# A DLRM tower with a two-layer interaction network: a top layer in two banks, a masked product, loads on two queues and a ninth pair of table products

## The chip, the cores and the metric

The kernel runs on one core of one Trainium2 chip. The metric is the device time of one execution in microseconds (us). Before the change the median of three runs is 152.55 us (152.45 to 153.67).

## The reference

For each of 512 samples, 26 embedding rows of 32 numbers are looked up. Two interaction layers follow, each a sum over pairs of fields, then three dense layers:

```
e  = stack(tbl_f[ids[:, f]] for f in 0..25)                  # 512 x 26 x 32
x1 = einsum('bik,bjk,hij->bhk', e,  e, W1) + b1              # W1: 128 x 26 x 26
x2 = einsum('bik,bjk,hij->bhk', x1, e, W2) + b2              # W2: 128 x 128 x 26
z  = concat(sum_k x1, sum_k x2)                              # 512 x 256
h  = relu(concat(z, dense_ctx) @ W_top1 + b_top1)            # 272 -> 512
h  = relu(h @ W_top2 + b_top2)                               # 512 -> 256
y  = h @ W_top3                                              # 256 -> 1
```

## The kernel before

The batch is cut into four groups (g = 0 to 3) of 128 samples. The network is linear in its weights, so both layers are folded: once, at the start, weight tables are mixed into `v_in`, `v_ac` (for x2) and `wg` (for x1), and then each group only needs products of field pairs and triples, contracted with these tables.

**At the start.** SyncE's queue loads the indices, W2 and W1, index copies for a one-hot form (`octet`, 125 partitions), eight small embedding tables (`small_tbl`, 125 partitions each, four for fields of the second half, four for the first half), the context rows of the top layer eight times (`wt1c_in`, line 314) and the dense weights, in the order in which `sync` writes them (lines 302 to 318). VectorE clears buffers, splits the context (lines 366 to 378) and the context weights (`split_wt1c`, line 599) into three bf16 parts, prepares W1's tables (lines 383 to 409), and turns the index copies into one-hot matrices (`one_hot`, `one_hot_rest`). TensorE computes 26 products W2 x W1 (`mix`, line 667), ScalarE copies each out of PSUM.

**Embeddings.** GpSimd gathers one field of one group per indirect DMA (line 350), 88 in all, in the order of groups and fields. Fields in `OH_PAIRS` are not gathered: a pair of fields of a small table is looked up by TensorE as one-hot x table (`look_up`, line 714), then VectorE masks and sums the result (`pick`, line 519), two instructions a pair. `OH_AT` puts the look-ups of group g+1 behind two places of group g's transposed products; pairs beyond two come after the last of them.

**A group.** VectorE's `build_a` and `build_b` transpose the embeddings (`take_part`), copy them to `l`, multiply pairs, and fill `R` (`fill_r`, line 550), a block-diagonal form of the same numbers: each of four quarters of 32 partitions has its own slot. For groups 0 and 1 ScalarE fills `R` instead. `l` and `R` have one buffer, so `build_a` of a group waits for the products of the group before. TensorE's `t_block` (lines 684 to 712) contracts `l` with `R`, eight matmul blocks and then four more, into a ring of four PSUM banks; ScalarE copies each to `t_in` or `t_ac`. Then `z_group`: 26 products `inner` (line 746) on `t_in`, 13 products `across` (line 751) on `t_ac`, and `gram_part` (line 734), four products for x1. The operand of `gram_part` makes a detour: SyncE's queue writes rows of `t_in` to DRAM and reads them back as `gram` (lines 320 to 331) after the first eight blocks are copied out.

**The top.** ScalarE copies the two halves of z out of PSUM (`z_copy`), TensorE runs `layer1` (lines 786 to 794: four blocks m of 128 outputs, three matmuls each, all in bank `h1p`), ScalarE applies ReLU per block (`relu1`), TensorE runs `layer2` and, one block of the next group later, `layer3`. On TensorE `layer1` and `layer2` of group g stand between `z_group` of g and the first `t_block` of g+1. ScalarE's order in between is `z_copy(0)`, `fill_r(1, 1)`, `relu1(0)`, `fill_r(1, 2)` for group 0, and without the fills later.

Of the kernel before, what the change touches and what calls it, by code (L numbers as in the profile page):

```python
# [16 lines left out]
BF16 = mybir.dt.bfloat16  # L17
# [4 lines left out]
P = 128  # L22
NF = 26
# [47 lines left out]
OH_PAIRS = ((0, 13, 17), (0, 18, 22), (1, 3, 5), (1, 13, 17), (2, 3, 5), (2, 8, 10), (3, 3, 5), (3, 8, 10))  # L71
# [5 lines left out]
OH_FIRST, OH_FIRST_AT = 2, 18  # L77
# [18 lines left out]
def build(nc, a, y):  # L96
    with ExitStack() as ctx:
# [6 lines left out]

        idx = sb("idx", [P, G, NF], I32)
# [38 lines left out]
        wt1c_mid = sb("wt1c_mid", [P, D1], BF16)  # L144
# [46 lines left out]
        zeroed = sem("zeroed")  # L191
        gap_zeroed = sem("gap_zeroed")
# [37 lines left out]
        pre = [("ctx", 0, 0), ("small", 0, 0)]  # L230
        pre += [("mix", x, 1) for x in range(NF)]
# [29 lines left out]
        def bank_free(kind, n):  # L261

            i = turn_of[kind, n] - RING
            if i < 0:
                return None
            old, m = turns[i]
            return {"pre": pre_out, "t": t_out, "z1": z1_ready, "oh": picked_out}[old], m + 1

# [32 lines left out]
        def _(sp):  # L301
            sp.dma_start(idx[:, :, :], a["ids"].rearrange("(g p) f -> p g f", p=P)).then_inc(ids_in, 16)
            sp.dma_start(w2t[:, :, :], a["L0_rec_W2"]).then_inc(w2_in, 16)
            sp.dma_start(w1[:, :, :], a["L0_rec_W1"]).then_inc(w1_in, 16)
            sp.dma_start(octet[0:OR, 0:OH_FIRST, :, :], a["octet_ids"][:, 0:OH_FIRST, :, :]).then_inc(octet_first, 16)
            sp.dma_start(place_in[:, :, :], a["place_ids"]).then_inc(place_loaded, 16)
# [8 lines left out]
            sp.dma_start(octet[0:OR, OH_FIRST:NP, :, :], a["octet_ids"][:, OH_FIRST:NP, :, :]).then_inc(octet_rest, 16)  # L315
# [40 lines left out]
        def _(dve):  # L356

            dve.memset(ctx_x[:, :, :, :], 0.0).then_inc(ctx_split, 1)
            for c in range(2):
# [5 lines left out]
            dve.memset(t_ac[P // 4:HALF, :, :], 0.0).then_inc(gap_zeroed, 1)  # L365
            dve.wait_ge(ctx_loaded, 16)
            x = ctx_in
            for n, part in enumerate(("hi", "mid", "lo")):
                dve.tensor_copy(ctx_part[:, :, :], x[:, :, :]).then_inc(ctx_split, 1)
                dve.wait_ge(ctx_split, 2 * n + 2)  # L370
                for s in range(SLOTS):
                    if CTX_SLOTS[s] == part:
                        last = dve.tensor_copy(ctx_x[:, :, s, :], ctx_part[:, :, :])
                if n < 2:
                    last = dve.tensor_tensor(ctx_rest[n][:, :, :], x[:, :, :], ctx_part[:, :, :], ALU.subtract)
                    x = ctx_rest[n]
                last.then_inc(ctx_split, 1)
                dve.wait_ge(ctx_split, 2 * n + 3)

            dve.memset(R[:, 0:NT // 2, :, :], 0.0)  # L380


# [26 lines left out]
            dve.tensor_copy(w1g[:, NH * NF:GR].rearrange("p (u v) -> p u v", v=NH), w1[:, NH:NF, NH:NF]).then_inc(w1_ready, 1)  # L409

# [139 lines left out]
            def fill_r(g, part):  # L550
# [3 lines left out]
                if g in R_ACT:  # L554
                    return
                f0, f1 = PARTS[part]
# [59 lines left out]
            one_hot()  # L616
            split_wt1c()
            one_hot_rest()
# [19 lines left out]
        def _(pe):  # L638
# [8 lines left out]
            def prepare(n):  # L647
# [4 lines left out]
                if kind == "small":  # L652
                    pe.wait_ge(rows_in, 16 * 5)
                    last = pe.transpose(ps[:, 0:10], rows[:, :], ident[0:10, 0:10])
                elif kind == "ctx":
                    keep_warm(WARM_CTX, h1p[:, 0, :])
# [85 lines left out]
            def z_group(g, first, tail=False):  # L742
# [11 lines left out]
                if first:  # L754
                    pe.wait_ge(t_out, TB * (g + 1))
                    pe.wait_ge(pre_out, LATE)
                    across(start=True)
                    for n in range(LATER, len(pre)):
                        prepare(n)
# [3 lines left out]
                    look_up(1, 1)  # L763
# [4 lines left out]
                inner(0, NF, start=True)  # L768
                pe.wait_ge(t_out, TB * (g + 1))
                if not tail:  # L770
                    across(stop=True).then_inc(z2_done, 1)
                    gram_part(g)
                    return
# [12 lines left out]
            def layer1(g):  # L786
                pe.wait_ge(z1_ready, g + 1)
# [218 lines left out]
```

## Time and profile before

| | us |
|---|---|
| median of 3 runs (range) | 152.55 (152.45 to 153.67) |
| the profiled execution | 151.98 |
| its span in the profile | 150.2 |
| TensorE matmuls busy | 129.0 (86%) |
| VectorE busy | 103.0 (69%) |
| ScalarE busy | 73.9 (49%) |
| GpSimd busy | 87.8 (58%) |

Busy shares are means over stages. From 0 to about 51 us the tables are made and the first group is built, VectorE working through a long list; from there to 148.6 us TensorE is nearly always busy. The mean granted clock of TensorE is 0.966 of full speed; it stands at half from about 8 to 18 us.

### The profile page before, as it was taken

What the parts mean: (1) busy time and instruction counts of PE and PEld (TensorE: products, weight loads), DVE (VectorE), ACT (ScalarE), POOL (GpSimd) and SP (SyncE); (2) the same over time, 40 slices, a digit from 0 to 9 for tenths busy, and PEclk for the clock granted to TensorE, in tenths of its full rate; (3) what the DMA queues carried; (4) which work ended last, traced back from release to release, by engine and by line L of the source; (5) the groups of instructions that cost most, each with busy time, mean ns of one, the idle gap of its engine ahead of it and who ended that gap; (6) DMA issues with size and microseconds to landing.
All of it is one profiled execution on the core that took longest, in us unless ns stands there. A gap on an engine that the chain in (4) does not pass through costs nothing.

```text
span 150.2 us, 5238 instructions
## 1 busy us (share of the span) xinstructions
PE 129.0 (86%) x2218; PEld 114.3 (76%) x2218; DVE 103.0 (69%) x351; ACT 73.9 (49%) x201; POOL 87.8 (58%) x96
## 2 busy tenths in 40 slices
PE   5335999983988689988999998899999889699994
PEld 5323666753987579988879998887999877599992
DVE  7889583999999999789159969937994993000000
ACT  1220488487767874718658401363930146590042
POOL 3787777777788777777777777777777100000000
PEclk9955599999999999999999999999999999999999
DMA  6976438620013130100103220011332000311000
GB/s 116 387 157 176 117 135 213 194 74 20 13 18 59 40 82 13 18 13 13 18 18 61 72 54 13 14 18 18 60 83 48 5 0 4 52 45 54 0 0 1
DMA packets 9065, 9.36 MB, mean 62 GB/s; under 512 B 3089, under 2 KB 8047, under 8 KB 8862
## 3 DMA queue, kind: packets, MB, share of 16 engines
q1 hardware_dynamic: 5678, 7.55, 17.5%
q0 software_dynamic: 2816, 1.45, 7.1%
q8 instruction: 17, 0.28, 0.8%
q10 hardware_dynamic: 548, 0.04, 0.3%
q14 instruction: 6, 0.05, 0.1%
HBM read 7.99 MB, written 1.04 MB: 60 GB/s over the span
## 4 chain that ended last, share of the span: by engine, by line
PE 60%; DVE 17%; SPq 8%; DMA 7%; ACT 3%; issue 3%; DVEq 0%
PE h2y L746 16%; PE h2y L751 8%; DMA octet<-in_octet_ids 7%; PE ring L702 7%; PE ring L710 5%; DVE l L569 5%; PE h2y L801 5%; SPq L310 3%; SPq L314 3%; PE ring L730 3%; PE ring L680 2%; PE ring L739 2%; PE h1p L792 2%; DVE vh_in L443 2%; PE ring L703 2%
## 5 line engine op out<-in xcount | busy, mean ns | idle before, releaser
L350 POOL DMA_INDIRECT emb<-in_tbl,idx x88 | 86.9, 988 | 28.2 <-issue 26.5
L746 PE MATMUL h2y<-t_in,v_in 128*128 128x128 f32 x208 | 24.3, 276 | 0.0
L746 PEld LDWEIGHTS h2y<-t_in,v_in 128*128 128x128 f32 x208 | 23.7, 192 | 0.2
L667 PE MATMUL ring<-w1s,w2t 128*128 128x352 f32 x52 | 18.3, 515 | 3.5 <-DVE w1s L404 3.5
L912 ACT COPY t_in<-ring 128x416 f32<-128x416 f32 x32 | 15.2, 537 | 11.3 <-PE ring L703 11.3
L702 PEld LDWEIGHTS ring<-r,l 64*64 64x64 f32 x512 | 16.4, 134 | 4.5 <-issue 2.1
L702 PE MATMUL ring<-r,l 64*64 64x52 f32 x512 | 18.1, 220 | 1.6 <-issue 1.2
L667 PEld LDWEIGHTS ring<-w1s,w2t 128*128 128x128 f32 x52 | 11.1, 215 | 9.9 <-DVE w1s L404 3.6
L703 PE MATMUL ring<-r,l 64*64 64x52 f32 x512 | 18.3, 220 | 0.0
L703 PEld LDWEIGHTS ring<-r,l 64*64 64x64 f32 x512 | 16.5, 134 | 0.0
L569 DVE TENSOR_TENSOR l<-sg_b,l 128x192 f32<-128x192 f32 (+5 forms) x72 | 16.1, 299 | 0.2
L569 DVE TENSOR_TENSOR l<-sg_a,l 128x192 f32<-128x192 f32 (+5 forms) x72 | 15.8, 298 | 0.1
L711 PE MATMUL ring<-r,l 128*42 128x52 f32 x256 | 13.2, 209 | 2.1 <-issue 2.1
L710 PEld LDWEIGHTS ring<-r,l 128*42 128x42 f32 x256 | 12.4, 117 | 2.8 <-issue 2.4
L927 ACT ACTIVATE z<-h2y,kb 128x128 f32<-128x128 f32 x4 | 1.5, 368 | 24.4 <-PE h2y L751 21.0
L710 PE MATMUL ring<-r,l 128*42 128x52 f32 x256 | 13.3, 209 | 0.0
L711 PEld LDWEIGHTS ring<-r,l 128*42 128x42 f32 x256 | 12.4, 117 | 0.0
L751 PE MATMUL h2y<-t_ac,v_ac 106*128 106x128 f32 x104 | 12.3, 275 | 0.0
L878 ACT COPY w_room<-ring 128x141 f32<-128x141 f32 x26 | 7.2, 278 | 9.7 <-PE ring L667 8.1
L751 PEld LDWEIGHTS h2y<-t_ac,v_ac 106*128 106x128 f32 x104 | 11.9, 192 | 0.0
L897 ACT COPY r<-l 32x416 f32<-32x416 f32 (+2 forms) x24 | 10.5, 437 | 1.3 <-DVE l L548 1.0
L919 ACT COPY t_ac<-ring 42x416 f32<-42x416 f32 x16 | 8.0, 500 | 2.0 <-PE ring L711 1.7
(133 smaller groups left out, 209.5 us busy)
## 6 DMA issues: line engine op xcount, KB each, us to landing
w2t<-in_L_rec_W SPq DMA_DIRECT2D x1, 1664.0 KB, 7.0
emb<-in_tbl,idx POOLq DMA_INDIRECT x88, 3.0
wt<-in_W_top SPq DMA_DIRECT2D x2, 512.0 KB, 8.8
small_tbl<-in_tbl SPq DMA_DIRECT2D x8, 125.0 KB
octet<-in_octet_ids SPq DMA_DIRECT2D x1, 750.0 KB
gram_scratch<-t_in SPq DMA_DIRECT2D x4, 169.0 KB
gram<-gram_scratch SPq DMA_DIRECT2D x4, 126.0 KB
w<-in_L_rec_W SPq DMA_DIRECT2D x1, 338.0 KB, 7.3
```

The costliest lines, as they stand in the source:

```text
L350: pool.indirect_dma_start(out=emb[:, g, f * K:(f + 1) * K], out_offset=None, in_=a[f"tbl_{f}"][:, :], in_offset=bass.IndirectOffsetOnAxis( ...
L569: last = dve.tensor_tensor(lc(c, col, n), sgt[c][:, :, q:q + n], lc(c, SGL + p, 1).to_broadcast([P, NT, n]), ALU.mult)
L667: last = pe.matmul(ps[:, 0:PR + MIX], w2t[:, c, :], w1_of[c // NH], start=True, stop=True)
L702: pe.matmul(banks[h][0:HALF, s], l[r, t, 0:HALF], fields, start=True, stop=True)
L703: last = pe.matmul(banks[h][HALF:P, s], l[r, t, HALF:P], fields, start=True, stop=True)
L710: pe.matmul(ps[0:NX, s], l[:, t, P:P + NX], R[:, t, :, NH:NF], start=True, stop=True)
L711: last = pe.matmul(ps[HALF:HALF + NX, s], l[:, t, P + NX:LW], R[:, t, :, 0:NH], start=True, stop=True)
L746: last = pe.matmul(z2p, v_in[:, j, :], t_in[:, j, :], start=(start and j == j0), stop=(stop and j == j1 - 1))
L751: last = pe.matmul(z2p, v_ac[0:MC, j, :], t_ac[0:MC, j, :], start=(start and j == 0), stop=(stop and j == NH - 1))
L897: last = act.copy(R[s, :, q, f0:f1], lc(c, SGL + o, w)[s, :, :])
L912: act.copy(t_in[:, :, :].rearrange("p j (t q) -> p j t q", q=4)[:, :, t0:t0 + BLK, 2 * h:2 * h + 2], ps[:, 0:BLK * 2 * NF].rearrange("p (t ...
L919: act.copy(t_ac[0:NX, :, s], src[0:NX, :, :])
```

## The change

- **Top layer one.** `layer1` now begins block 0 (in `h1p`) and block 2 (in a ring bank of its own, a new turn `h1`) before the second half of z is there, closes blocks 0 and 1, signals ScalarE, then closes 2 and 3 in the other bank and signals again. `relu1` waits for each half.
- **z order.** In groups 1 and 2 `gram_part` moves ahead of `across`, and ScalarE copies the x1 half of z first. In group 0 the look-up of group 1's second pair moves ahead of `inner`.
- **R.** Where VectorE fills R (groups 2 and 3), four copies of 32 partitions become one product of all 128 partitions with a 0/1 mask `sample_of`, written into all four quarters.
- **Loads.** SyncE's queue takes W1 ahead of W2; the index copies (`octet` in two pieces, `place_ids`) go to ScalarE's queue. VectorE prepares W1's tables before it splits the context and clears R; `one_hot_rest` comes before `split_wt1c`. The context transposes on TensorE move behind the ninth `mix`. `wt1c_mid` lives in a part of `t_in`.
- **Ninth pair.** Fields 13 and 17 of group 2 are looked up by one-hot; GpSimd's gathers go from 88 to 86.

```diff
-OH_PAIRS = ((0, 13, 17), (0, 18, 22), (1, 3, 5), (1, 13, 17), (2, 3, 5), (2, 8, 10), (3, 3, 5), (3, 8, 10))
+OH_PAIRS = ((0, 13, 17), (0, 18, 22), (1, 3, 5), (1, 13, 17), (2, 3, 5), (2, 8, 10), (2, 13, 17), (3, 3, 5), (3, 8, 10))
...
-        turns += [("pre", n) for n in range(LATE, len(pre))] + [("z1", 0)]
+        turns += [("pre", n) for n in range(LATE, len(pre))] + [("z1", 0), ("h1", 0)]
...
-            turns += [("z1", g)]
+            turns += [("z1", g)] + ([("h1", g)] if g < G - 1 else [])
...
             sp.dma_start(idx[:, :, :], a["ids"].rearrange("(g p) f -> p g f", p=P)).then_inc(ids_in, 16)
+            sp.dma_start(w1[:, :, :], a["L0_rec_W1"]).then_inc(w1_in, 16)
             sp.dma_start(w2t[:, :, :], a["L0_rec_W2"]).then_inc(w2_in, 16)
-            sp.dma_start(w1[:, :, :], a["L0_rec_W1"]).then_inc(w1_in, 16)
-            sp.dma_start(octet[0:OR, 0:OH_FIRST, :, :], a["octet_ids"][:, 0:OH_FIRST, :, :]).then_inc(octet_first, 16)
-            sp.dma_start(place_in[:, :, :], a["place_ids"]).then_inc(place_loaded, 16)
...
-            sp.dma_start(octet[0:OR, OH_FIRST:NP, :, :], a["octet_ids"][:, OH_FIRST:NP, :, :]).then_inc(octet_rest, 16)
...
+            act.dma_start(octet[0:OR, 0:OH_FIRST, :, :], a["octet_ids"][:, 0:OH_FIRST, :, :]).then_inc(octet_first, 16)
+            act.dma_start(octet[0:OR, OH_FIRST:NP, :, :], a["octet_ids"][:, OH_FIRST:NP, :, :]).then_inc(octet_rest, 16)
+            act.dma_start(place_in[:, :, :], a["place_ids"]).then_inc(place_loaded, 16)
...
-                for q in range(4):
-                    s = slice(K * q, K * (q + 1))
-                    last = dve.tensor_copy(R[s, :, q, f0:f1], sgt[c][s, :, o:o + w])
-                last.then_inc(r_ready, 1)
+                form = [P, NT, 4, w]
+                dve.tensor_tensor(R[:, :, :, f0:f1], sgt[c][:, :, o:o + w].unsqueeze(2).to_broadcast(form),
+                                  sample_of[:, :].unsqueeze(1).unsqueeze(3).to_broadcast(form), ALU.mult).then_inc(r_ready, 1)
...
             one_hot()
+            one_hot_rest()
             split_wt1c()
-            one_hot_rest()
             build_a(0)
...
                 inner(0, NF, start=True)
+                if not tail:
+                    gram_part(g)
+                    pe.wait_ge(t_out, TB * (g + 1))
+                    across(stop=True).then_inc(z2_done, 1)
+                    return
...
             def layer1(g):
+                out = h1_of(g)
...
                 pe.wait_ge(z1_ready, g + 1)
+                pe.wait_ge(*bank_free("h1", g))
+                begin(0)
+                begin(2)
                 pe.wait_ge(z2_ready, g + 1)
-                for m in range(M1):
-                    s = slice(m * P, (m + 1) * P)
-                    pe.matmul(h1p[:, m, :], wt1c[:, s], ctx_t[:, g, :], start=True, stop=False)
-                    pe.matmul(h1p[:, m, :], wt1[:, 0, s], z[:, 0, :], start=False, stop=False)
-                    last = pe.matmul(h1p[:, m, :], wt1[:, 1, s], z[:, 1, :], start=False, stop=True)
-                last.then_inc(h1_done, 1)
+                close(0)
+                begin(1)
+                close(1).then_inc(h1_done, 1)
+                close(2)
+                begin(3)
+                close(3).then_inc(h1_done, 1)
...
-                z_copy(g, (1, 0))
+                z_copy(g, (0, 1))
```

Three places show how instructions move. The first is SyncE's queue at the start, before and after; `octet` is the index copies, `t_in` the eight loads of context weights.

```order
L302 DMA idx<-in_ids 128x4x26
L303 DMA w2t<-in_L_rec_W 128x3328
L304 DMA w<-in_L_rec_W 128x676
L305 DMA octet<-in_octet_ids 125x512
L306 DMA place_in<-in_place_ids 128x16
L310 DMA small_tbl<-in_tbl 125x256 x4
L314 DMA t_in<-in_W_top 16x512 x8
L315 DMA octet<-in_octet_ids 125x1536
L310 DMA small_tbl<-in_tbl 125x256 x4
```

```order
L310 DMA idx<-in_ids 128x4x26
L311 DMA w<-in_L_rec_W 128x676
L312 DMA w2t<-in_L_rec_W 128x3328
L316 DMA small_tbl<-in_tbl 125x256 x4
L320 DMA t_in<-in_W_top 16x512 x8
L316 DMA small_tbl<-in_tbl 125x256 x4
```

The two index copies, now 512 and 1792 elements a partition, and the places stand at the end of ScalarE's six small loads; the rest keeps its order.

The second is VectorE between group 1's products and group 2's build (L527/L531 before and L535/L539 after are the two instructions of a pick; STREAM_TRANSPOSE opens `build_a`).

```order
L527 TENSOR_TENSOR ctx_x<-ring,mask 128x512
L531 TENSOR_REDUCE emb<-ctx_x 128x2x32
L527 TENSOR_TENSOR ctx_x<-ring,mask 128x512
L531 TENSOR_REDUCE emb<-ctx_x 128x2x32
L543 STREAM_TRANSPOSE sg_a<-emb 128x13x32
```

```order
L535 TENSOR_TENSOR ctx_x<-ring,mask 128x512
L539 TENSOR_REDUCE emb<-ctx_x 128x2x32
L535 TENSOR_TENSOR ctx_x<-ring,mask 128x512
L539 TENSOR_REDUCE emb<-ctx_x 128x2x32
L535 TENSOR_TENSOR ctx_x<-ring,mask 128x512
L539 TENSOR_REDUCE emb<-ctx_x 128x2x32
L551 STREAM_TRANSPOSE sg_a<-emb 128x13x32
```

A third pick now stands ahead of group 2's first transpose.

The third is TensorE from the last block of group 1's transposed products to `layer2` (L801 before, L824 after), before and after.

```order
L746 MATMUL h2y<-t_in,v_in 128x128 x26
L751 MATMUL h2y<-t_ac,v_ac 128x128 x13
L739 MATMUL ring<-gram,wg 128x128 x4
L791 MATMUL h1p<-ctx_t,wt1c 128x128
L792 MATMUL h1p<-z,wt 128x128
L793 MATMUL h1p<-z,wt 128x128
```

```order
L739 MATMUL ring<-small_tbl,octet 128x256 x2
L755 MATMUL h2y<-t_in,v_in 128x128 x26
L748 MATMUL ring<-gram,wg 128x128 x4
L760 MATMUL h2y<-t_ac,v_ac 128x128 x13
L801 MATMUL h1p<-ctx_t,wt1c 128x128
L802 MATMUL h1p<-z,wt 128x128
L801 MATMUL ring<-ctx_t,wt1c 128x128
L802 MATMUL ring<-z,wt 128x128
L805 MATMUL h1p<-z,wt 128x128
```

The look-up of the third pair comes after the last transposed product; `gram_part` (L748) comes before `across` (L760).

## Rows read from the trace of the kernel before

**Rows 1.** Chain in order of time, start to table transposes (start us, us, what)
```profile
14.07 10.88 DMA octet<-in_octet_ids
...
26.98 0.55 DVE sg_a L543
...
51.13 0.63 PE ring L680 x4
```

**Rows 2.** Timeline, VectorE, start (start us, us, engine, line, operation [idle before <- releaser])
```profile
19.19 0.43 DVE L604 CAST wt1c<-t_in 128x512 bf16<-128x512 f32 x1 [2.17 <-DMA t_in<-in_W_top]
...
22.22 0.43 DVE L613 CAST wt1c<-t_in 32x512 bf16<-32x512 f32 x1
```

**Rows 3.** Window from the end of the first clears to `build_a(0)`, columns as in rows 4
```profile
4.50:26.98 22.48, 15.86 (x50) 10.06 (x50) 16.72 (x64) 10.35 (x44) 17.34 (x17) 0.77 0.68 198
```

**Rows 4.** Windows of one us: busy PE, PEld, DVE, ACT, POOL; clock, DMA share, GB/s
```profile
4.00:5.00 1.00, 1.00 (x9) 0.98 (x7) 0.62 (x2) 0.66 (x1) 0.69 (x2) 1.00 1.04 426
...
21.00:22.00 1.00, 1.00 (x5) 0.68 (x4) 0.96 (x2) 0.84 (x5) 0.69 (x2) 1.00 0.36 135
```

**Rows 5.** Timeline, GpSimd, the thirteenth gather; issue to landing of all gathers
```profile
18.96 0.95 POOL L350 DMA_INDIRECT emb<-in_tbl,idx  x1 [0.30 <-issue]
DMA to landing us min/median/max: 2.3/3.0/5.8
```

**Rows 6.** Timeline, ScalarE, between group 0 and group 1
```profile
67.20 2.06 ACT L897 COPY r<-l 32x352 f32<-32x352 f32 x4
69.86 1.14 ACT L932 ACTIVATE h<-h1p,cols 128x128 f32<-128x128 f32 x4 [0.61 <-PE h1p L793]
```

**Rows 7.** Chain in order of time, group 2's end to group 3
```profile
114.18 2.90 PE h2y L751 x26
117.08 0.91 PE ring L739 x8
...
118.67 0.28 PE h1p L792 x2
118.94 0.22 PE h1p L793 x2
...
123.45 0.19 PE ring L702
```

**Rows 8.** Timeline, VectorE, group 2's build
```profile
78.40 0.69 DVE L527 TENSOR_TENSOR ctx_x<-ring,mask 128x512 f32<-128x512 f32 x1 [0.37 <-PE ring L730]
80.30 0.63 DVE L543 STREAM_TRANSPOSE sg_a<-emb 128x416 f32<-128x416 f32 x1
84.13 2.38 DVE L561 COPY r<-sg_a 32x416 f32<-32x416 f32 x4
89.92 0.56 DVE L543 STREAM_TRANSPOSE sg_b<-emb 128x352 f32<-128x352 f32 x1 [1.44 <-DMA emb<-in_tbl,idx]
90.96 2.11 DVE L561 COPY r<-sg_b 32x352 f32<-32x352 f32 x4
96.12 0.92 DVE L561 COPY r<-sg_b 32x64 f32<-32x64 f32 x4
```

**Rows 9.** Chain in order of time, group 1's end and group 2's start
```profile
77.30 1.06 PE ring L730 x4
82.68 6.00 PE h2y L746 x52
97.95 0.19 PE ring L702
```

**Rows 10.** Groups by shape, VectorE products: busy, mean ns of one
```profile
L565 DVE TENSOR_TENSOR l<-sg_a,l 128x416 f32<-128x416 f32 x4 | 2.4, 593 | 0.1
L443 DVE TENSOR_TENSOR vh_ac<-mix 128x546 f32<-128x546 f32 x2 | 2.3, 1172 | 0.0
```

**Rows 11.** Window at the end of group 2's gram reads, columns as in rows 4
```profile
114.00:115.00 1.00, 1.00 (x11) 1.00 (x10) 0.00 (x0) 0.00 (x0) 0.70 (x2) 1.00 0.09 21
```

**Rows 12.** Timeline, VectorE, group 3's second part
```profile
116.08 0.56 DVE L543 STREAM_TRANSPOSE sg_b<-emb 128x352 f32<-128x352 f32 x1 [2.11 <-DMA emb<-in_tbl,idx]
```

More of the change, by code:

```diff
@@ L76 @@
 R_ACT = (0, 1)
-OH_FIRST, OH_FIRST_AT = 2, 18
+OH_FIRST, OH_FIRST_AT, CTX_AT = 2, 18, 9
 T_AT = tuple(range(0, NB, 2)) + tuple(range(NB, TB))
@@ L191, in build @@
         zeroed = sem("zeroed")
+        sample_mask = sem("sample_mask")
         gap_zeroed = sem("gap_zeroed")
@@ L228, in cut @@
             return [(j, min(most, count - j)) for j in range(0, count, most)]
-        pre = [("ctx", 0, 0), ("small", 0, 0)]
-        pre += [("mix", x, 1) for x in range(NF)]
+        pre = [("small", 0, 0)]
+        pre += [("mix", x, 1) for x in range(CTX_AT)] + [("ctx", 0, 0)] + [("mix", x, 1) for x in range(CTX_AT, NF)]
         pre += [("wg", 0, 0)]
@@ L266, in bank_free, with h1_of @@
             old, m = turns[i]
+            if old == "h1":
+                return h1_ready, M1 * (m + 1)
             return {"pre": pre_out, "t": t_out, "z1": z1_ready, "oh": picked_out}[old], m + 1
+        def h1_of(g):
+            return [h1p[:, 0, :], h1p[:, 1, :]] + [bank_of("h1", g)[:, m * P:(m + 1) * P] for m in range(2)]
         def pick_bank(g, n):
@@ L358, in _ @@
             dve.memset(ctx_x[:, :, :, :], 0.0).then_inc(ctx_split, 1)
+            dve.memset(sample_of[:, :], 0.0).then_inc(sample_mask, 1)
+            dve.wait_ge(sample_mask, 1)
+            for q in range(4):
+                last = dve.memset(sample_of[K * q:K * (q + 1), q:q + 1], 1.0)
+            last.then_inc(sample_mask, 1)
             for c in range(2):
@@ L364, in _ @@
             dve.memset(vh_ac[:, :, NX:HALF], 0.0)
[L365 to L380, printed above, removed]
             dve.wait_ge(w1_in, 16)
@@ L409, in _ @@
             dve.tensor_copy(w1g[:, NH * NF:GR].rearrange("p (u v) -> p u v", v=NH), w1[:, NH:NF, NH:NF]).then_inc(w1_ready, 1)
+            dve.wait_ge(ctx_loaded, 16)
+            x = ctx_in
+            for n, part in enumerate(("hi", "mid", "lo")):
+                dve.tensor_copy(ctx_part[:, :, :], x[:, :, :]).then_inc(ctx_split, 1)
+                dve.wait_ge(ctx_split, 2 * n + 2)
+                for s in range(SLOTS):
+                    if CTX_SLOTS[s] == part:
+                        last = dve.tensor_copy(ctx_x[:, :, s, :], ctx_part[:, :, :])
+                if n < 2:
+                    last = dve.tensor_tensor(ctx_rest[n][:, :, :], x[:, :, :], ctx_part[:, :, :], ALU.subtract)
+                    x = ctx_rest[n]
+                last.then_inc(ctx_split, 1)
+                dve.wait_ge(ctx_split, 2 * n + 3)
+            dve.memset(t_ac[P // 4:HALF, :, :], 0.0).then_inc(gap_zeroed, 1)
+            dve.memset(R[:, 0:NT // 2, :, :], 0.0)
             def mixed(c, x0, x1, quarters):
@@ L555, in fill_r @@
                     return
+                if g == G - 2 and part == 0:
+                    dve.wait_ge(sample_mask, 2)
                 f0, f1 = PARTS[part]
@@ L757, in z_group @@
                     across(start=True)
+                    look_up(1, 1)
                     for n in range(LATER, len(pre)):
@@ L768, in z_group @@
                 inner(0, NF, start=True)
+                if not tail:
[3 more added lines that the diff above has]
+                    return
                 pe.wait_ge(t_out, TB * (g + 1))
[L770 to L773, printed above, removed]
                 across(stop=True).then_inc(z2_done, 1)
@@ L786, in layer1, with begin, close @@
             def layer1(g):
+                out = h1_of(g)
+                def begin(m):
+                    s = slice(m * P, (m + 1) * P)
+                    pe.matmul(out[m], wt1c[:, s], ctx_t[:, g, :], start=True, stop=False)
+                    pe.matmul(out[m], wt1[:, 0, s], z[:, 0, :], start=False, stop=False)
+                def close(m):
+                    return pe.matmul(out[m], wt1[:, 1, m * P:(m + 1) * P], z[:, 1, :], start=False, stop=True)
                 pe.wait_ge(z1_ready, g + 1)
+                pe.wait_ge(*bank_free("h1", g))
+                begin(0)
+                begin(2)
                 pe.wait_ge(z2_ready, g + 1)
-                for m in range(M1):
-                    s = slice(m * P, (m + 1) * P)
-                    pe.matmul(h1p[:, m, :], wt1c[:, s], ctx_t[:, g, :], start=True, stop=False)
-                    pe.matmul(h1p[:, m, :], wt1[:, 0, s], z[:, 0, :], start=False, stop=False)
-                    last = pe.matmul(h1p[:, m, :], wt1[:, 1, s], z[:, 1, :], start=False, stop=True)
-                last.then_inc(h1_done, 1)
+                close(0)
[4 more added lines that the diff above has]
+                close(3).then_inc(h1_done, 1)
             def layer2(g, out, tail=False):
```

12 lines of the change are left out of this document (6 added, 6 removed).

## Prediction

> **What bounds the kernel now.** I read the chain of waits first, then the timelines of the engines that it names, then windows for the DMA side. All sums are against the profiled execution, 151.98 us (span 150.2); the median of the runs is 0.57 us above it, which I don't add, since their range is 1.2 us wide.
>
> The chain has two halves. Until 51.13 us it is a load and then VectorE: `octet`'s rest is issued at 14.07 and lands at 24.95, the one-hot form of it takes VectorE to 26.98, where `build_a(0)` starts, and from there VectorE works without a gap until the folded tables are ready for TensorE at 51.13 [rows 1]. Whatever moves the start of `build_a(0)` moves that hand-over by as much. I call this shift D. The second half is TensorE, group after group. It is not alone there. Group 2's last fill of R ends at 96.12 + 0.92 = 97.04, and TensorE starts on group 2 at 97.95 [rows 8, 9]: VectorE has 0.9 us in hand, no more. Inside group 2 VectorE also waits 1.44 us for gathers, in group 3 2.11 us [rows 8, 12].
>
> **1. The front (D).** Removed: the idle times before `split_wt1c` (2.17 us) [rows 2] and the wait for `octet`. Added: index copies for one more pair, 125 partitions x 256 numbers x 4 bytes, 125 KB. Changed: `octet` no longer waits in SyncE's queue, but `split_wt1c` now stands behind the one-hot work and directly ahead of `build_a(0)`, and it lasts from 19.19 to 22.22 + 0.43 = 22.65, 3.46 us [rows 2].
>
> The question is what limited these loads: the queue they stood in, or the DMA engines. W2's load ran at 426 GB/s with all 16 engines busy (share 1.04), the copies at 135 GB/s with share 0.36 [rows 4]. The rate fell with the share of busy engines, to about 135/426 = a third; the few engines in use, some six of 16 with the gathers, ran near full rate. Then a second queue adds nothing for the same kind of load: what had to pass before (two octet copies, 1000 KB, four tables of 125 KB, the context weights) still has to pass ahead of `split_wt1c`, which waits for the context weights behind the four tables, while the copies take turns from ScalarE's queue. That is the same set plus 125 KB, 0.9 us at 135 GB/s: the last of it lands at 24.95 + 0.9 = 25.9 instead of 24.95. If the context weights are last, the split runs to 25.9 + 3.46 = 29.4 and D = 29.4 - 26.98 = +2.4. I take this end: small rows of the tables against large rows of the copies, turn by turn, should let the copies through first.
>
> The Trainium skill ("DMA: Bandwidth & Descriptors", "Why a DMA increments its semaphore by 16 and not by 1") says that a load uses the largest number up to 16 that divides its partitions, so 125 partitions go over 5 engines, and ("Issuing engines are not separate DMA queues") that two issuing engines share the same DMA engines. By that rule D is positive as above; by the opposite reading, that one queue gave only 135 GB/s, it is the gain of the third rival. The share in the windows agrees with the rule; that both queues use the same five no row shows.
>
> Bounds of D. High: the copies land last; then the mask (0.7, an estimate from its three small instructions), the one-hot rest (26.98 - 24.95 = 2.0) and the split all follow 25.9: 32.1, D = +5.1. Low: nothing is shared; then the thirteenth gather, 18.96 + 3.0 = 22.0 [rows 5], and VectorE's own list are what is left. From 4.50 to 26.98 that list was 16.72 us of work in 64 instructions [rows 3]; with 0.3 for the wider one-hot rest and, an estimate, 1 us of gaps, and W1 landed at about 4.9 (it now moves first), it ends at 22.9: D = -4.1.
>
> Clearing, the W1 tables and the context split only change places in that list; they lie ahead of `split_wt1c`'s wait and cost nothing as long as the loads are last (with them gone as cover, the 22.9 above is the floor). W1 ahead of W2 starts the `mix` products earlier; VectorE needs them only after `build_b(0)`, so they earn nothing, and the moved context transposes lie in the same slack.
>
> **2. Layer one, group 0.** z's second half is copied, then ScalarE has `fill_r(1, 1)` until 67.20 + 2.06 = 69.26, and only then its ReLUs, which started at 69.86 [rows 6]. So of the earlier `layer1` only 0.6 us arrives: **-0.6**. The look-up moved ahead saves VectorE a wait in group 1, where VectorE isn't last.
>
> **3. Ninth pair, group 1 to 2.** TensorE now does the third look-up after its last transposed product, where `inner` began: 82.68 + 1.06 [rows 9]. VectorE masks it only then. From mask to the first transpose took 80.30 - 78.40 = 1.90 [rows 8], so `build_a(2)` starts at 82.68 + 1.06 + 0.04 + 1.90 = 85.68 in the old clock instead of 80.30, 5.38 later. Against it: the wait for gathers of 1.44 is gone (two gathers less are 2 x (0.95 + 0.30) = 2.5 us [rows 5]), and the masked product. A product from PSUM takes 593 ns for 416 elements [rows 10] and 0.69 us for 512 [rows 8], about 1.03 ns for each further element; the three products have 1664, 1408 and 256 elements, so 1.88 + 1.61 + 0.42 = 3.9 us in place of 2.38 + 2.11 + 0.92 = 5.4 [rows 8]: -1.5. The dear end is the strided 546-element sum, 1172 ns [rows 10] or 2.15 ns an element, 7.1 us for all 3328, +1.7. The source runs of 13 are contiguous, so I take the cheap end. R is full at 97.04 + 5.38 - 1.44 - 1.5 = 99.48, against 97.95 when TensorE started: **+1.5**. TensorE's own gain in group 1's `layer1` (below, 1.5) falls into this wait.
>
> **4. Group 2 to 3.** From `inner`'s end to the next group took 123.45 - 114.18 = 9.27 us [rows 7]. Now `gram_part` follows `inner`. Its operand was still being read at 21 GB/s up to 115 [rows 11], and had landed by 117.08, where the products began without a wait [rows 7]; I put the landing at 116.0, between the two, a wait of 1.8 us that `across` used to hide. Then 0.91 for the gram products, 2.90 for `across`; two begun blocks 2 x 0.28 (they hide the copy of z), two times 0.22 + 0.28 + 0.22 for the rest [rows 7], and `layer2` at 2.0 (eight products of 0.22, paced by the last two ReLUs): 1.8 + 0.91 + 2.90 + 0.56 + 1.44 + 2.0 = 9.61, **+0.3**. Without the wait it would be -1.5.
>
> By the same page's rule the first gram read, 127 partitions, has only one DMA engine, so this tail can't be shortened by an emptier chip; 21 GB/s in the window agrees. VectorE in group 3 has more than 2 us in hand, so its cheaper fill earns nothing there; nor do the earlier gathers, whose floor for group 3 is 116.08 - 2.5 = 113.6 and 6.1 us of building (7.1 as in group 2, less 1.0 of the masked product): 119.7, while TensorE comes at 127. The last group's tail isn't changed.
>
> **Sum.** 2.4 - 0.6 + 1.5 + 0.3 = +3.6: 151.98 + 3.6 = **155.6 us**.
>
> **Rivals.**
> - *The copies last, or a dear mask product.* D = +5.1 gives 158.3; the dear product adds 3.2 to the forecast, 158.8. For it: the tables for the first half stand behind the context weights and can take turns with the copies; against: the product's runs are contiguous. 15%.
> - *The front comes out even.* The window of 426 GB/s shows what an engine can do; some of the 9 us between 16 and 25 may have been gaps that two queues fill. With 2.4 us regained D = 0 and the time is 153.2. 15%.
> - *Two queues carry side by side* (faster). The limit of 135 GB/s was the queue's; copies and context weights land before 20, D = -4.1, and the rest of the sum stays: 151.98 - 4.1 + 1.2 = 149.1. Group 3 then starts at 120.6, still above the floor of 119.7 that the gathers set. It decides the sign as soon as D is under -1.2. For it: SyncE's queue did stand between issue at 14.07 and landing; against: the share of 0.36. 25%.
> - The forecast, D between +1 and +4: 154 to 157.5. 45%.
>
> **Range and chances.** The measurement tells about 1% from no change, so faster is under 151.0 and slower over 154.1. Slower: nearly all of the forecast (0.43), the first rival (0.15), a little of the second: 0.60. Faster: the third, 0.25. Same: 0.15. Cases of both signs need a wide range, 148.9 to 158.5; the forecast's own is 154 to 157.5.
>
> **What would show it.** `split_wt1c` ending at about 29.4 with a DMA wait before it, and `build_a(0)` right behind: step 1. If the wait is before the one-hot rest, the first rival; if there is none and VectorE waits for gathers near 22, the third. ReLUs of group 0 beginning right at the end of `fill_r(1, 1)`: step 2. TensorE idle about 1.5 us ahead of group 2 with VectorE's fill as releaser, and masked products of 1.9, 1.6 and 0.4 us: step 3. TensorE idle 1.8 us ahead of the gram products of group 2: step 4. I am wrong if `octet` and the context weights land before 22.

## The result, and the profile after

The changed kernel takes **156.69 us** (median of 6 runs, 155.82 to 158.19); the kernel before took 152.69 us on the same chip (6 runs). The ratio is 1.023, with a 95% interval of 1.0183 to 1.0276: slower by 3.5 us by the ratio, by 4.0 by the medians. An execution more than 1.5% above the fastest of its kernel (one of the six here, one of 25 of the kernel before, two of ten in run 8, two of six in run 12) is left out of every ratio and interval in this document, while the medians take in all. The profiled execution has a span of 154.5 us against 150.2 (+4.3), and the time is followed through these two. The table sets the places where the chain of waits passes from one part to the next beside each other.

| start of (us) | before | after | shift | step, measured | step, forecast |
|---|---|---|---|---|---|
| `build_a(0)` | 26.98 | 30.00 | +3.0 | front +3.0 | +2.4 |
| group 1 on TensorE | 72.44 | 74.97 | +2.5 | layer one, group 0: -0.5 | -0.6 |
| group 2 | 97.95 | 101.62 | +3.7 | group 1 to 2: +1.1 | +1.5 |
| group 3 | 123.45 | 127.3 | +3.9 | group 2 to 3: +0.2 | +0.3 |
| end of the span | 150.2 | 154.5 | +4.3 | the rest +0.4 | 0 |

**The front.** The chain of the kernel after, in order of time (start us, us, what), answers to [rows 1]:

```profile
18.87 7.61 DMA t_in<-in_W_top
26.50 0.44 DVE wt1c L613
...
29.54 0.43 DVE wt1c L622
30.00 0.64 DVE sg_a L551
```

It no longer runs over `octet` but over the context weights, and the split of these stands in it whole. VectorE's timeline of the same stretch, as [rows 2]:

```profile
22.59 0.17 DVE L512 TENSOR_SCALAR place_in<-place_in 128x18 int32<-128x18 int32 x1 [5.98 <-DMA place_in<-in_place_ids]
23.35 1.09 DVE L498 TENSOR_SCALAR octet<-octet 125x1792 int32<-125x1792 int32 x1
24.48 1.15 DVE L501 TENSOR_SCALAR octet<-octet,iota_pf 125x1792 f32<-125x1792 int32 x1
26.50 0.43 DVE L613 CAST wt1c<-t_in 128x512 bf16<-128x512 f32 x1 [0.87 <-DMA t_in<-in_W_top]
```

VectorE stands idle for 5.98 us until the places land behind the copies in ScalarE's queue, then works on the one-hot form, waits 0.87 us more for the context weights, and splits them for 3.46 us. The windows (busy PE, PEld, DVE, ACT, POOL; clock, DMA share, GB/s) answer to [rows 4]:

```profile
4.00:5.00 1.00, 1.00 (x8) 1.00 (x7) 0.99 (x5) 0.47 (x1) 0.69 (x2) 1.00 0.95 353
21.00:22.00 1.00, 1.00 (x4) 0.59 (x4) 0.00 (x0) 0.84 (x5) 0.88 (x1) 1.00 0.41 123
```

With two queues the loads run at 123 GB/s and a share of 0.41, where one queue gave 135 and 0.36: the second queue brought nothing at this place, nor from 10 to 25 us as a whole (a mean of 136 GB/s against 154). The chain shows one more thing: SyncE's queue issued the last of the eight context loads only at 18.87, against 13.61 before, and one of these issues took 6.90 us.

**Group 0 to 1.** The chain, where before the ReLUs had a wait [rows 6]: 

```profile
71.84 0.52 ACT r L924
72.40 0.38 ACT h L959
72.77 0.04 issue
72.82 2.15 PE h2y L824 x16
74.97 0.19 PE ring L711
```

`relu1` begins at the end of `fill_r(1, 1)`, with no idle time between.

**Group 1 to 2.** VectorE's timeline (as [rows 8]) and TensorE's (the chain was in [rows 9]):

```profile
86.39 0.69 DVE L535 TENSOR_TENSOR ctx_x<-ring,mask 128x512 f32<-128x512 f32 x1 [3.70 <-PE ring L739]
88.08 0.61 DVE L551 STREAM_TRANSPOSE sg_a<-emb 128x416 f32<-128x416 f32 x1
91.89 1.88 DVE L570 TENSOR_TENSOR r<-sg_a,sample_of 128x1664 f32<-128x1664 f32 x1
95.55 0.54 DVE L551 STREAM_TRANSPOSE sg_b<-emb 128x352 f32<-128x352 f32 x1
96.57 1.61 DVE L570 TENSOR_TENSOR r<-sg_b,sample_of 128x1408 f32<-128x1408 f32 x1
101.11 0.41 DVE L570 TENSOR_TENSOR r<-sg_b,sample_of 128x256 f32<-128x256 f32 x1
```

```profile
86.19 5.97 PE L755 MATMUL h2y<-t_in,v_in 128*128 128x128 f32 x52
93.08 1.16 PE L748 MATMUL ring<-gram,wg 127*128 127x128 f32 x8 [0.93 <-DMA gram<-gram_scratch]
94.08 3.07 PE L760 MATMUL h2y<-t_ac,v_ac 106*128 106x128 f32 x26
99.26 2.26 PE L824 MATMUL h2y<-h,wt 128*128 128x128 f32 x16
101.62 0.23 PE L711 MATMUL ring<-r,l 64*64 64x52 f32 x1
```

The third pick, the three masked products (1.88, 1.61 and 0.41 us) and the vanished gather wait are as forecast. New is a 0.93 us wait for gram already in group 1. R is full at 101.52, and `layer2` ends at 101.52: two limits fall on one point, and this profile alone can't tell which holds group 2.

**Group 2 to 3**, TensorE's timeline, where before `across` ran first [rows 7]:

```profile
118.87 1.16 PE L748 MATMUL ring<-gram,wg 127*128 127x128 f32 x8 [0.96 <-DMA gram<-gram_scratch]
```

The wait is 0.96 us, not 1.8. The last 0.4 us of the span lie in two gaps of "issue" in group 3's blocks, 0.95 and 1.40 us where before there were 0.36 and 1.43. I know no cause for them, and they need not come from the change: from group 3's first product to the end the same instructions took 27.2 us here, 26.8 before, and 26.1 to 27.1 in the profiles of the twelve runs below.

### The profile page after: what moved, and what is told of

Its sections match the earlier page's. It is cut to its first block, busy times and chain, and to the rows that moved or that the text cites. A ratio compares the mean times of both kernels' runs of the same rounds, so it can differ in the third digit from the quotient of the medians.

```text
span 154.5 us, 5237 instructions
## 1 busy us (share of the span) xinstructions
PE 131.5 (85%) x2222; PEld 116.4 (75%) x2222; DVE 101.5 (66%) x340; ACT 74.0 (48%) x201; POOL 85.1 (55%) x94
## 4 chain that ended last, share of the span: by engine, by line
PE 45%; DVE 19%; DMA 15%; SPq 14%; ACT 3%; issue 3%; DVEq 0%
PE h2y L755 8%; PE h2y L760 8%; SPq L320 7%; PE ring L711 6%; DMA gram<-gram_scratch 5%; DVE l L578 5%; DMA t_in<-in_W_top 5%; DMA gram_scratch<-t_in 5%; PE h2y L824 5%; SPq L316 3%; PE ring L739 3%; PE ring L748 3%; SPq L333 2%; PE ring L712 2%; PE ring L689 2%
## 5 line engine op out<-in xcount | busy, mean ns | idle before, releaser
L355 POOL DMA_INDIRECT emb<-in_tbl,idx x86 | 84.2, 979 | 27.7 <-issue 25.9
L720 PE MATMUL ring<-r,l 128*42 128x52 f32 x256 | 13.4, 210 | 1.8 <-issue 1.8
L719 PE MATMUL ring<-r,l 128*42 128x52 f32 x256 | 13.4, 210 | 0.0
L760 PE MATMUL h2y<-t_ac,v_ac 106*128 106x128 f32 x104 | 12.3, 275 | 0.0
L760 PEld LDWEIGHTS h2y<-t_ac,v_ac 106*128 106x128 f32 x104 | 11.9, 192 | 0.0
L739 PE MATMUL h1p<-small_tbl,octet 125*128 125x256 f32 x12 | 4.2, 481 | 8.5 <-DVE emb L539 8.0
L535 DVE TENSOR_TENSOR ctx_x<-ring,mask 128x512 f32<-128x512 f32 x5 | 3.5, 691 | 11.3 <-PE ring L739 11.3
```

The source lines that it names most:

```text
L355: pool.indirect_dma_start(out=emb[:, g, f * K:(f + 1) * K], out_offset=None, in_=a[f"tbl_{f}"][:, :], in_offset=bass.IndirectOffsetOnAxis( ...
L719: pe.matmul(ps[0:NX, s], l[:, t, P:P + NX], R[:, t, :, NH:NF], start=True, stop=True)
L720: last = pe.matmul(ps[HALF:HALF + NX, s], l[:, t, P + NX:LW], R[:, t, :, 0:NH], start=True, stop=True)
L760: last = pe.matmul(z2p, v_ac[0:MC, j, :], t_ac[0:MC, j, :], start=(start and j == 0), stop=(stop and j == NH - 1))
```

## The experiments

My theory: the front costs 3 us because the loads end as late as ever and the split of the context weights now stands behind them; the ninth pair and the late operand of the gram products take back what layer one and the z order give. The rival for the front was that the order in the queues is at fault and not the DMA engines; for the groups, that one of the two terms is a mere shadow of the other. "Start of group g" below is TensorE's first product with R. Runs 1 to 4, 5 to 8 and 9 to 12 were made in three batches; each ratio is against executions of the kernel before in the same batch (medians 152.36, 152.58 and 152.15 us).

**1. The front alone** (the kernel before, with the change's loads, its order on VectorE and its place for the context transposes; eight pairs):

```diff
-            sp.dma_start(octet[0:OR, 0:OH_FIRST, :, :], ...
-            sp.dma_start(place_in[:, :, :], a["place_ids"]).then_inc(place_loaded, 16)
...
+            act.dma_start(octet[0:OR, 0:OH_FIRST, :, :], ...
+            act.dma_start(octet[0:OR, OH_FIRST:NP, :, :], ...
+            act.dma_start(place_in[:, :, :], a["place_ids"]).then_inc(place_loaded, 16)
...
+            one_hot_rest()
             split_wt1c()
-            one_hot_rest()
```

> The kernel before with the change's front alone: W1 ahead of W2, the index copies and the places on ScalarE's queue, W1's tables ahead of the context split, the one-hot rest ahead of the split of the context weights, context transposes behind the ninth mix. Main theory (the loads of 125 partitions share a few DMA engines whatever the queue, and the split of the context weights now waits for all of them): build_a(0) starts about 3 us later than the 26.98 of before (a little less than the 30.00 of the changed kernel, since 125 KB of copies are not there) and the time is 155.0 to 155.7. Rival (the front is neutral and the layer and the ninth pair cost the time): build_a(0) within 1 us of 27, time 152.5 to 153.5. Rival (ScalarE's issues delay its first copies and with them the mix products): the mix products, not a load, end last before build_a(0).

Measured: 154.88 us, ratio 1.0171 [1.0097, 1.0245]; `build_a(0)` at 29.62, groups 1 to 3 at 75.1, 100.6 and 126.1. The shift of 2.7 goes through to the end unchanged. The front alone makes a slower kernel, 0.1 us under the expected range.

**2. The change with the front of before** (nine pairs; the same edit backwards).

> The changed kernel with the front of before (load order, queues and VectorE's order at the start), the layer in two banks, the masked product, the z order and the ninth pair kept. Main theory: build_a(0) back near 27, the rest of the change costs 1.0 to 1.5 us: 153.4 to 154.0. The octet load is 125 KB larger than before, so up to 0.9 us may remain on top. Rival (the cost is in the ninth pair and the gram order): 155.5 or more.

Measured: 153.78 us, ratio 1.0108 [1.0028, 1.0188], inside the expected range; `build_a(0)` at 27.68, 0.7 later than before. VectorE's timeline shows two parts of it:

```profile
25.48 1.10 DVE L501 TENSOR_SCALAR octet<-octet 125x1792 int32<-125x1792 int32 x1 [3.54 <-DMA octet<-in_octet_ids]
26.61 1.15 DVE L504 TENSOR_SCALAR octet<-octet,iota_pf 125x1792 f32<-125x1792 int32 x1
```

The copies land at 25.48 instead of 24.95, and the rest takes 0.2 us more. The 0.2 are the wider one-hot form, the ninth pair's price. The 0.5 would fit its 125 KB, but they aren't shown to come from them: run 9, with eight pairs and the same loads as before, has its copies at 25.75 and `build_a(0)` at 27.68 as well, so the landing of the same loads moves by 0.8 us between executions. In the new order the three profiles with nine pairs (the change, runs 4 and 8) have the context weights at 26.50, 26.10 and 26.75, the three with eight (runs 1, 5 and 6) at 26.32, 26.23 and 26.38. So of D = 3.0 nearly all is the new order and queue: with eight pairs it is 2.6 to 2.8 against the profile before, and still 1.9 to 2.1 against run 9. TensorE then waits 0.72 us for VectorE ahead of group 2 (first product at 99.25, `layer2` done at 98.53), the wait that step 3 forecast; the gram wait of group 1 is only 0.30 us here.

**3. Loads over more engines.** The change, with each load of 125 partitions cut into 120 and 5:

```diff
+CUTS = ((0, 120), (120, OR))
...
+                    for r0, r1 in CUTS:
+                        sp.dma_start(small_tbl[r0:r1, i, :], ...
...
+            for r0, r1 in CUTS:
+                act.dma_start(octet[r0:r1, 0:OH_FIRST, :, :], ...
```

> The changed kernel with each load of 125 partitions (two index copies, eight tables) issued as 120 partitions and 5. Same bytes, same queues, ten more issues. Main theory (125 partitions go over 5 DMA engines, 120 over 15): the copies, places and context weights land before 17, the split ends near 23, build_a(0) starts at 22.5 to 24 instead of 30.00, and the time is 149 to 150.5. Rival (the limit is a queue, its descriptors or DRAM): the loads land at 22 to 26 as before, time 156 to 157; the extra issues could even delay the context weights.

Measured: 150.83 us, ratio 0.9894 [0.9819, 0.9968], 0.3 us over the expected range. A window in which both kernels load the copies (the change, then run 3; columns as in rows 4), and run 3's VectorE:

```profile
12.00:14.00 2.00, 2.00 (x5) 1.14 (x4) 1.45 (x1) 0.99 (x4) 1.39 (x3) 0.50 0.49 130
12.00:14.00 2.00, 2.00 (x4) 1.05 (x4) 1.49 (x2) 0.97 (x4) 1.38 (x3) 0.50 0.94 214
```

```profile
17.91 0.37 DVE L514 TENSOR_SCALAR place_in<-place_in 128x18 int32<-128x18 int32 x1 [1.33 <-DMA place_in<-in_place_ids]
21.07 0.42 DVE L615 CAST wt1c<-t_in 128x512 bf16<-128x512 f32 x1
24.97 0.63 DVE L553 STREAM_TRANSPOSE sg_a<-emb 128x416 f32<-128x416 f32 x1 [0.63 <-DMA emb<-in_tbl,idx]
```

The same kind of load now moves at 214 GB/s with a share of 0.94, the places land 4.7 us earlier, VectorE waits for none of these loads behind them, and `build_a(0)` starts 5.0 us earlier, now at the gathers. SyncE has issued all eight context loads by 9 us. That decides the question of the front: the limit was the few engines, not the queue. Nor can it be that each load was merely issued as two: the pieces of 5 partitions hold 4% of the bytes, too few to add two thirds to the rate by moving beside the rest. It is what the Trainium skill states ("DMA: Bandwidth & Descriptors", "Why a DMA increments its semaphore by 16 and not by 1"): the engines in use are the largest number up to 16 that divides the partitions, so by its rule 5 for 125 and 15 for 120. The trace agrees: a share of 0.49 with gathers beside, against 0.94.

**4. The gram read over more engines.** The change, with the first read of 127 rows cut:

```diff
-                for i in range(2):
-                    sp.dma_start(gram[0:GCH[i], i, :], gram_dram[GOFF[i]:GOFF[i] + GCH[i], :]).then_inc(gram_in, 16)
+                for i, r0, r1 in ((0, 0, 112), (0, 112, GCH[0]), (1, 0, GCH[1])):
+                    sp.dma_start(gram[r0:r1, i, :], gram_dram[GOFF[i] + r0:GOFF[i] + r1, :]).then_inc(gram_in, 16)
```

> The changed kernel with the first gram read, 127 rows, issued as 112 rows and 15. Main theory (127 rows go through one DMA engine, the 21 GB/s tail): gram lands some 2 us earlier, TensorE's wait ahead of the gram products (0.93 us in groups 1 and 2) is gone; in group 1 VectorE's R is full only at 101.5, so nothing is won there, in group 2 0.9 us: 155.6 to 156.0. Rival (the round trip through DRAM sets the landing, not the read's engine): no difference, 156.7, the wait stays.

Measured: 154.93 us, ratio 1.0188 [1.0108, 1.0269], an interval that overlaps that of the change. By the trace:

```profile
91.64 1.06 PE L748 MATMUL ring<-gram,wg 127*128 127x128 f32 x8
101.25 0.23 PE L711 MATMUL ring<-r,l 64*64 64x52 f32 x1 [1.28 <-DVE l L578]
```

No wait for gram is left, TensorE is done with group 1 at 99.98, and still waits 1.28 us for VectorE. So VectorE, late by the third pick, holds group 2, and the gram wait of group 1 was only its shadow. Group 2 starts 0.4 us earlier, less than the 0.6 by which this execution's front was early. Group 3 starts at 125.64 instead of 127.25: 1.6, of which 1.2 arise behind the start of group 2; 0.96 of them are the gram wait that is gone, 0.1 the gram products (1.06 for 1.16). The median came out 0.7 us under the expected 155.6 to 156.0.

**5. Without the ninth pair** (`(2, 13, 17)` taken out of `OH_PAIRS`).

> The changed kernel with eight pairs of table products, the ninth (group 2, fields 13 and 17) taken out; everything else kept. Theory A (two limits of equal length stand between group 1 and group 2: VectorE's fill of R, late through the third pick, and gram, landing 10 us after its source is copied out and needed ahead of the z products): only the first goes, gram still lands at about 93, TensorE's idle time before the gram products grows from 0.9 to about 2 us, group 2 starts within 0.4 us of before and the time is 156.2 to 157.0. Theory B (the third pick alone costs the 1.1 us): 155.0 to 155.6.

Measured: 155.16 us, ratio 1.014 [1.0041, 1.024]. `build_a(2)` starts at 82.90, 5.2 earlier, but groups 2 and 3 only 0.7 and 0.5 earlier (100.88, 126.74). The median came out below the 156.2 to 157.0 of the theory and inside the 155.0 to 155.6 of the rival, that the pick alone costs the 1.1 us; with an interval of 1.5 us to either side it doesn't choose. The trace stands between the two: group 2 gained 0.7, where the theory allowed 0.4, and the gram wait grew only to 1.21 us, where it said 2. But the wait grew, as only the theory has it. TensorE's timeline names it:

```profile
92.50 1.16 PE L748 MATMUL ring<-gram,wg 127*128 127x128 f32 x8 [1.21 <-DMA gram<-gram_scratch]
```

**6. Both together**, no ninth pair and the cut gram read.

> The changed kernel with eight pairs and the first gram read issued as 112 rows and 15. Both limits between group 1 and 2 are gone. Theory A: group 2 starts 2.2 to 2.6 us earlier than in the changed kernel, group 3 another 0.9, 153.0 to 153.8, more than the sum of the two single edits (about 0 and about 1 to 1.8). Theory B: the sum of the single edits, 154 or so for a gain of 1.1 on top of the split gram read.

Measured: 152.81 us (10 runs), ratio 1.0015 [0.9973, 1.0056]; groups 2 and 3 at 100.00 and 124.77, 1.6 and 2.5 us ahead of the change, while the edits alone gave 0.4 and 0.7 at group 2. The executions also differ ahead of group 1 (here it starts at 75.34, 0.4 us later than in the change; the last section has the clock beside it), so the fair measure starts there: from group 1's start to group 2's it took 26.7 us in the change, 26.6 in run 4, 25.9 in run 5 and 24.7 here. Gains of 0.1 and 0.8 alone, 2.1 together: each edit alone uncovers the other's limit. With both, the group part of the change earns what the late front costs. The time is 0.2 us under the expected range.

**7. The work in the other order.** The change, with the context weights loaded ahead of the tables and split ahead of the one-hot work:

```diff
-            load_tables(OH_B, small_b_in)
             for s in range(SLOTS):
                 sp.dma_start(wt1c_in[s * CTX:(s + 1) * CTX, :], ...
+            load_tables(OH_B, small_b_in)
...
+            split_wt1c()
             one_hot()
             one_hot_rest()
-            split_wt1c()
```

> The changed kernel with the eight loads of the context weights ahead of the four tables on SyncE's queue, and their split ahead of the one-hot work on VectorE. Same bytes on the same two queues. Main theory (the split of 3.5 us stood behind the last load): it now runs near 15 to 19 beside the loads; places land at 22 to 23, the one-hot rest ends near 25.6 and build_a(0) starts at 25.5 to 26.5, 4 us earlier than in the changed kernel: 152.3 to 153.2. Rival (the loads themselves are later, order does not matter): build_a(0) at 29 to 30, 156 or more.

Measured: 151.32 us (10 runs), ratio 0.9905 [0.9859, 0.9951]. VectorE:

```profile
15.62 0.36 DVE L613 CAST wt1c<-t_in 128x512 bf16<-128x512 f32 x1
...
22.40 0.18 DVE L512 TENSOR_SCALAR place_in<-place_in 128x18 int32<-128x18 int32 x1 [2.32 <-DMA place_in<-in_place_ids]
...
25.36 0.62 DVE L551 STREAM_TRANSPOSE sg_a<-emb 128x416 f32<-128x416 f32 x1
```

The places land as late as in the change (22.40 against 22.59), yet `build_a(0)` starts 4.6 us earlier: the split has moved under the wait for the loads, which shrinks from 5.98 to 2.32. The time fell 1.0 us below the expected range: of the 5.8 us between the two spans 4.6 are there at `build_a(0)` and 1.1 come from the last group (26.1 us against 27.2), which this edit doesn't touch. So the front has two independent cures, loads that end sooner and work that doesn't stand behind them.

**8. The third look-up behind the eighth block**, with the cut gram read (`OH_AT = (3, 5, 7)`).

> The changed kernel with the third look-up of a group behind block 7 of the transposed products instead of behind the last (OH_AT = (3, 5, 7)) and the first gram read as 112 rows and 15. Theory A: the pick ends about 2.5 us earlier, VectorE's R is full about 99, TensorE comes later than that, so group 2 starts when TensorE is ready, about 1.5 us earlier than in the changed kernel with the split read alone (101.5 to 100), group 3 as with the split: 153.3 to 154.0. Rival (VectorE still sets group 2, since build_a waits for block 7 anyway): 154.9, no gain over the split read.

Measured: 154.26 us (10 runs), ratio 1.0061 [1.0013, 1.0109]. `build_a(2)` starts at 85.93, 2.2 earlier than in the change, but group 1 at 76.05, 1.1 later, and that is not the look-up's doing, since neither edit touches anything ahead of group 1. The rows of slices (granted clock in tenths) of this kernel:

```profile
PEclk9955999996559999999999999999999999999999
```

After an idle time of 7.88 us TensorE starts on group 0 at 39.40, and the granted clock stands at 0.50 (1.2 GHz) up to 45, where in the change it did up to 42. Its blocks then end so late that the chain goes over them to 57.54, where in the change it goes over VectorE to 56.52. The gain of the pick and the loss by the clock lie in one number; the run doesn't settle the look-up. Runs 11 and 12 do.

**9. The group part by itself**: the change with the front of before, no ninth pair, and the cut gram read.

> The change without its front and without its ninth pair, and with the first gram read in two pieces: what the group part of the change is worth when nothing is taken back. Theory A (the front costs 3.0 us, the pair and the late gram operand take back what layer one and the z order give): against the kernel with the changed front and the same other edits (152.8 us) it gains the front's 2 to 3 us: build_a(0) near 27.5, group 2 near 98, group 3 near 122.5, time 150.0 to 151.0. Rival B (the group part earns nothing of its own, VectorE and the gathers are behind everything): as before, 152.4 to 153.

Measured: 150.90 us, ratio 0.9883 [0.9834, 0.9932]. `build_a(0)` at 27.68, group 3 at 122.60, 0.8 us ahead of before from a start 0.7 behind: layer one in two banks, the z order and the masked product are worth about 1.5 us once nothing takes them back. Both time and places lie in the expected ranges.

**10. to 12. The cures together.** Run 10 is the change with the cuts of run 3, the order of run 7, the cut gram read and no ninth pair; run 11 the same with the ninth pair; run 12 is run 11 with its look-up behind the eighth block:

```diff
-OH_AT = (3, 5)
+OH_AT = (3, 5, 7)
```

> The change with every 125-partition load cut into 120 and 5, context weights loaded and split first, the first gram read as 112 and 15, and no ninth pair. Theory A (the four costs add up): build_a(0) near 24.5 to 25, group 1 near 70, group 2 near 95, group 3 near 120 to 120.5, where the gathers of group 3 set the floor (two gathers more than with nine pairs): 147.5 to 149.0 us. Rival B (the gathers become the bound, since GpSimd starts no earlier than before): group 3 late with a gather wait ahead of its second part, 149.5 to 151.

> As the kernel without the ninth pair of the same call, but with nine pairs. Theory A: the third pick puts group 2 about 1 us later, group 3 about 0.5 to 0.8 later: 148.3 to 149.8 us. Rival B (the gathers are the bound once the front is earlier, and two fewer of them pay): 0.5 to 1 us faster than with eight pairs.

> As the nine-pair kernel of the same call, with the third look-up behind the eighth block of transposed products instead of behind the last. Theory A (VectorE's late pick was what held group 2): pick and build_a(2) about 1.5 to 2 us earlier, group 2 up to 1 us earlier: 147.5 to 149.0 us, at or under the kernel with eight pairs. Rival B (as with the late front, the look-up there disturbs the ring and the groups before start later): no gain, 149 to 150.

| | us | ratio | `build_a(0)` | groups 1, 2, 3 |
|---|---|---|---|---|
| 10 | 148.97 | 0.978 [0.9742, 0.9818] | 24.14 | 69.0, 93.4, 120.15 |
| 11 | 149.81 | 0.9819 [0.9779, 0.986] | 25.31 | 70.5, 97.1, 121.6 |
| 12 | 148.08 | 0.9692 [0.9641, 0.9743] | 24.58 | 69.5, 94.8, 119.4 |

All three beat both kernels, and what bounds each differs. VectorE and TensorE in run 10:

```profile
114.06 0.56 DVE L553 STREAM_TRANSPOSE sg_b<-emb 128x352 f32<-128x352 f32 x1 [5.15 <-DMA emb<-in_tbl,idx]
```

```profile
120.15 0.23 PE L713 MATMUL ring<-r,l 64*64 64x52 f32 x1 [1.88 <-DVE l L580]
```

TensorE in run 11, and VectorE in run 12:

```profile
97.12 0.23 PE L713 MATMUL ring<-r,l 64*64 64x52 f32 x1 [1.29 <-DVE l L580]
```

```profile
112.09 0.56 DVE L553 STREAM_TRANSPOSE sg_b<-emb 128x352 f32<-128x352 f32 x1 [1.81 <-DMA emb<-in_tbl,idx]
```

With eight pairs the gathers have become the limit: VectorE waits 5.15 us for them in group 3, and TensorE 1.88 us for VectorE (the rival expected this, the time is still the theory's). Nine pairs put group 2 3.7 us later in run 11, 1.2 of it from its front, where the theory said about 1, and its time stands at the edge of the expected range. With nine pairs, two gathers fewer, but a late pick, it is VectorE ahead of group 2, 1.29 us. With nine pairs and the early look-up `build_a(2)` starts at 79.38 instead of 83.58, TensorE waits for neither, and group 3 starts 2.2 us ahead of run 11, 0.7 of them from its front. By its ratio run 12 is 4.7 us faster than the kernel before (4.1 by the medians), and the best found.

## Why the prediction was right, and where not

- **Step 1, the front, +2.4 forecast, +3.0 measured.** Three parts held: the limit by engines (run 3), the context weights last, and the 3.46 us split behind them with `build_a(0)` directly behind that (run 7). The term that was off is the landing, 26.50, not 25.9, and here the closeness is in part luck. I priced only the added copies, at 0.9 us, and the new order at nothing, as "the same set". The runs show it the other way round: without the added copies the context weights landed at 26.23 to 26.38 (runs 1, 5, 6), 1.3 to 1.4 us behind the 24.95, and with them at 26.10 to 26.75, 0.1 us later on average. Which loads take turns to make the delay I haven't shown; the late issue at 18.87 is all that the rows say. The rival of two queues side by side was refuted by the share, and its cure was right beside it: the same trace that showed 0.36 said that spreading the load would pay.
- **Step 2, layer one in group 0, -0.6 forecast, -0.5 or -0.6 measured** (2.53 against 3.02 at `build_a(0)`, or 3.13 at the end of `inner`).
- **Step 3, +1.5 forecast, +1.1 measured.** The pick (86.39, that is 83.86 with group 1's shift of 2.53 taken off, against 83.78 worked out) and the products were right. From `build_a(2)` to the full R it took 13.4 us where the terms gave 13.8. What I had left out is that the gram wait, which I priced only for group 2, comes in group 1 too: it ate 0.93 us of TensorE's gain of 1.5, so the sign that I had named, 1.5 us of idle TensorE ahead of group 2, is absent. It cost nothing here since VectorE was as late (run 4), but it is why taking the pair out gives so little (run 5), and both together so much more (run 6).
- **Step 4, +0.3 forecast, +0.2 measured**, with a wait of 0.96 instead of 1.8: the operand landed at 118.83, 0.9 us after `inner`'s end, where I had chosen a point 1.8 us after it, between two bounds of 0.8 and 2.9. The rest of the layer took 0.6 more than summed, 0.25 of it in the gram products (1.16 for 0.91).
- **The sum** gave +3.6 where the spans differ by 4.3. It is short by 0.6 at the front and by 0.4 in stalls of the last group, which lie within what that group varies by, and it is over by 0.4 in group 1 to 2; these errors partly cancel. The median of 156.69 against 155.6 adds the 0.4 us by which the profiled execution is below it.
- The floor of group 3 by gathers, 119.7 with nine pairs, stood close: run 12 reached 119.4, with 1.8 us of gather wait on VectorE; with eight pairs the gathers took over (run 10).

## What to carry to other kernels

Before a load is moved to another queue, look at the share of the DMA engines while it runs. Here a low share with a low rate meant that the load's shape limits it, and the cure was to cut it along the partitions, not to move it. Work that needs no late load belongs ahead of the wait for one, however short the wait looked where it stood. And where two edits each leave the next limit within a microsecond, test them in a pair too: measured from group 1's start, these were worth 0.1 and 0.8 us alone, 2.1 together. And before a delay of half a microsecond is given a cause, look how far the same loads move between executions: 0.8 us here.

## What the runs showed of the hardware

- 125 partitions against 120 and 5: 130 GB/s and a share of 0.49, against 214 GB/s and 0.94, from 12 to 14 us.
- A load of 9 KB (the places) landed at 22.59, behind 1125 KB of copies ahead of it in the same queue. With the copies cut it landed at 17.91.
- Issuing a gather mostly took 0.94 us, but a few in each run took 1.1 to 2.2. The share of the DMA engines doesn't explain it: in run 3 one took 0.94 at 17.33 beside a share of 1.15 and the next 1.50 at 18.58 beside 1.02, and in the change one took 2.13 at 23.62 beside 0.61. What does is not shown.
- The granted clock fell to 0.50 a second time while TensorE was idle for 8.0 us (the change; look-ups of 2.05 us at 39.32, where run 3, not yet at half, has 1.10) and 7.9 us (run 8). After shorter idle times it fell in some executions (run 2, 2.6 us; run 3, 3.4 us, half from 36 to 38) and not in others (before, 2.9 us; run 7, 3.0 us; run 12, 2.1 us).
- Its cost went with the time at which it came back: from `build_a(0)` to group 1's start took 44.9 us in the change, where it was on its way up from 42, and 45.3 to 45.6 in runs 4 to 6, where it came back after 43. It took 46.0 in run 8, where it stayed at half up to 45. In the change VectorE's path hid it; in run 8 the late start of group 1, 1.1 us, is put down to it, which these five runs support and no run isolates.
